# A fused Perceiver kernel: another order of TensorE's work where two batches meet, and small products widened to the full array

## The reference, cut to what matters

```
x = layer_norm(image_embeds, ln1_g, ln1_b)      # 16 x 1601 x 128
l = layer_norm(latents, ln2_g, ln2_b)           # 16 x 64 x 128
q = l @ Wq;  kv_in = concat([x, l], axis=1);  k, v = split(kv_in @ Wkv)
w = softmax(q k^T * scale)                      # 16 heads, 64 x 1665 per head
out = (w @ v) @ Wo                              # back to 64 x 128
```

## Time and profile before

| | |
|---|---|
| Median of 3 runs | 1007.68 us (1007.14 to 1007.98) |
| Profiled execution, its own time | 1005.16 us |
| Its span, first to last instruction | 1003.4 us |
| TensorE busy | 936.7 us, 93% |
| VectorE busy | 760.4 us, 76% |
| ScalarE busy | 720.4 us, 72% |
| GpSimd busy | 376.7 us, 38% |
| Mean granted TensorE clock | 0.976 |

### The profile page before, as it was taken

One profiled execution on the slowest core, in us unless ns is written; L12 is line 12 of the kernel. 1 busy time (PEld: TensorE's weight loads), 2 busy tenths in 40 slices (PEclk: granted clock), 3 DMA queues, 4 the chain that ended last, 5 costly groups with the idle time before them and its releaser, 6 DMA issues.

```text
span 1003.4 us, 20455 instructions
## 1 busy us (share of the span) xinstructions
PE 936.7 (93%) x8246; PEld 488.8 (49%) x8246; DVE 760.4 (76%) x1556; ACT 720.4 (72%) x1033; POOL 376.7 (38%) x376
## 2 busy tenths in 40 slices
PE   8679999999999999999999999999999999979975
PEld 5434444444444444545454545454545444457752
DVE  5968796969696969696969696969695856568965
ACT  4577778787878787878787878787878676645631
POOL 6471133333433333333333334333333222244343
PEclk9799999999999999999999999999999999989987
DMA  6211030203120203020312031202120100000000
GB/s 203 68 27 52 12 79 13 78 13 78 14 76 15 77 15 75 16 75 17 74 18 72 19 73 17 74 18 73 18 61 18 39 2 22 1 23 23 2 6 16
DMA packets 74566, 41.95 MB, mean 42 GB/s; under 512 B 62277, under 2 KB 69865, under 8 KB 74473
## 3 DMA queue, kind: packets, MB, share of 16 engines
q1 hardware_dynamic: 74184, 39.60, 16.3%
q10 hardware_dynamic: 288, 1.05, 0.3%
HBM read 25.98 MB, written 0.59 MB: 26 GB/s over the span
## 4 chain that ended last, share of the span: by engine, by line
PE 56%; DVE 29%; ACT 8%; issue 5%; POOL 1%; DMA 1%; POOLq 0%; ACTq 0%; DVEq 0%
DVE mx L1457 8%; DVE region L1469 7%; PE S L2066 6%; PE WW L2012 6%; PE OA L2099 6%; PE S L2075 6%; PE S L2069 6%; PE OA L2102 6%; PE OA L2105 6%; DVE region L1448 4%; ACT S L1781 2%; ACT region L1777 2%; ACT region L1801 2%; PE WW L2039 1%; PE WW L2041 1%
## 5 line engine op out<-in xcount | busy, mean ns | idle before, releaser
L1469 DVE TENSOR_TENSOR region<-S,region 128x1024 f16<-128x1024 f32 x208 | 252.8, 1215 | 139.1 <-ACT S L1781 139.0
L1777 ACT ACTIVATE region<-S,sigma 128x1024 f16<-128x1024 f32 x208 | 232.6, 1118 | 131.6 <-PE S L2075 130.4
L1457 DVE TENSOR_REDUCE mx<-WW 128x1 f32<-128x512 f32 (+1 forms) x480 | 259.7, 584 | 42.0 <-PE WW L2012 37.6
L1781 ACT ACTIVATE S<-S,sigma 128x1024 f32<-128x1024 f32 x208 | 226.2, 1088 | 0.0
L2066 PE MATMUL S<-region,xT 128*128 128x512 f16 (+1 forms) x416 | 124.5, 381 | 6.0 <-DVE region L1469 4.7
L2012 PE MATMUL WW<-xT,region 128*128 128x512 f16 x360 | 121.3, 382 | 6.2 <-DVE region L1448 3.7
L2075 PE MATMUL S<-region,xT 128*128 128x512 f16 (+1 forms) x416 | 125.0, 382 | 0.0
L2099 PE MATMUL OA<-region,xk 128*128 128x512 f16 (+1 forms) x416 | 124.9, 382 | 0.0
L2102 PE MATMUL OA<-region,xk 128*128 128x512 f16 (+1 forms) x416 | 124.6, 381 | 0.0
L2069 PE MATMUL S<-region,xT 128*128 128x512 f16 (+1 forms) x416 | 124.5, 381 | 0.0
L2105 PE MATMUL OA<-region,xk 128*128 128x512 f16 (+1 forms) x416 | 123.8, 379 | 0.0
(11 more groups left out here) (310 smaller groups left out, 1783.3 us busy)
## 6 DMA issues: line engine op xcount, KB each, us to landing
raw<-ctx SPq DMA_DIRECT2D x16, 768.0 KB
rb<-inv_dram SPq DMA_DIRECT2D x16, 512.0 KB, 3.6
xT<-xk SPq DMA_TRANSPOSE x48, 3.1
left_row<-left_pT SPq DMA_DIRECT2D x48, 2.0 KB
raw<-ctx SPq DMA_DIRECT2D x16, 32.5 KB
WO_lo<-L_xattn_Wq ACTq DMA_DIRECT2D x1, 512.0 KB, 3.6
WO_hi<-L_xattn_Wkv ACTq DMA_DIRECT2D x1, 512.0 KB, 4.6
lx<-x SPq DMA_DIRECT2D x1, 512.0 KB, 6.5
```

The costliest lines, as they stand in the source:

```text
L1457: nc.vector.tensor_reduce(mx[:, r, c:c + 1], W[BANK[("m", n)]][:, 0:width], AX.X, ALU.max)\
L1469: nc.vector.tensor_tensor(p_lo[k], src, p_hi[k], ALU.subtract).then_inc(lo_done.sem, 1)
L1777: nc.scalar.activation(p_hi[k], src, ACT.Exp, scale=sigma[:, 0:1])
L1781: nc.scalar.activation(src, src, ACT.Exp, scale=sigma[:, 0:1]).then_inc(e_done.sem, 1)
```

## The change

TensorE's order where batches meet becomes: scores 12, `mt`, weigh 10, weigh 11 | scores 0 of the next batch, weigh 12 | scores 1, `pj` of the batch before the one just ended | scores 2, `lf`, weigh 0. So `pj` of batch b-2 stands in unit 1 of slot b instead of in unit 12 of slot b-1. `lf` and `lt` become early items (before `weigh`, not after), `lt` ahead of the two last `q`, and the side banks' parity moves with them. The copies of the side banks' outputs go from ScalarE in unit 1 to VectorE in unit 0, ahead of `low_part(b, 0)`. Four kinds of small products get full operands padded with zeros: `ones16` (1 x 64) becomes `first_row` (128 x 64, ones in row 0), `left_p` 128 x 128 instead of 128 x 16, `left_row` and `left_x` 128 rows instead of 3, and the weights of `mt` one column of `m16` repeated 128 times. VectorE clears the padding once, at the start. `queries_low`, the low halves of the queries, stays on VectorE. ScalarE's `outputs` and the latents' copies get an explicit wait for `o_split` of the batch before. The last slot keeps its own order in unit 12.

```diff
--- before.py
+++ after.py
@@ -87,19 +87,19 @@
 
 
 PLAN = [([], []),
-        ([], []),
-        ([], [("lf", 0)]),
+        ([], [("pj", 0)]),
+        ([("lf", 0)], []),
         ([("q", 0), ("q", 1)], some(0, 2)),
         (some(2, 2), some(4, 2)),
-        ([("q", 2), ("q", 3)], some(6, 1) + [("lt", 0)]),
+        ([("lt", 0), ("q", 2), ("q", 3)], some(6, 1)),
         (some(7, 2), some(9, 2)),
         (some(11, 2), some(13, 2)),
         (some(15, 2), some(17, 2)),
         (some(19, 2), some(21, 2)),
         (some(23, 2), some(25, 2)),
         (some(27, 2), some(29, 3)),
-        ([("mt", 0), ("mt", 1)], [("pj", 0)])]
-LATENTS_AT = 1
+        ([("mt", 0), ("mt", 1)], [])]
+LATENTS_AT = 0
 
 
 def bank_of_items():
@@ -140,7 +140,7 @@
         ident = sb("ident", [128, 128])
         ident16 = sb("ident16", [128, 128], F16)
         ones = sb("ones", [128, 128])
-        ones16 = sb("ones16", [1, 64], F16)
+        first_row = sb("first_row", [128, NQ], F16)
         rcol = sb("rcol", [128, 8])
         rinv = sb("rinv", [128, 8])
         rb = sb("rb", [128, COLS])
@@ -203,10 +203,10 @@
 
         left_s = sb("left_s", [128, 8])
         left_e = sb("left_e", [128, 8])
-        left_p = sb("left_p", [128, 16], F16)
+        left_p = sb("left_p", [128, 128], F16)
         left_pT = sb("left_pT", [16, 128], F16)
-        left_row = sb("left_row", [3, COLS], F16)
-        left_x = [sb(f"left_x{p}", [3, D], F16) for p in range(2)]
+        left_row = sb("left_row", [128, COLS], F16)
+        left_x = [sb(f"left_x{p}", [128, D], F16) for p in range(2)]
         srow = sb("srow", [1, COLS])
         attnT = sb("attnT", [128, B * NQ])
 
@@ -489,6 +489,13 @@
             eng.wait_ge(oa_free.sem, oa_free.upto(turn))
             eng.wait_ge(free["ol"].sem, free["ol"].upto(turn, 1))
             vec.tensor_tensor(srow[:], o_sb[0:1, 0, :], o_sb[0:1, 1, :], ALU.add).then_inc(srow_done.sem, 1)
+
+        def latent_outputs(eng, copy, turn):
+            eng.wait_ge(pv_done.sem, pv_done.upto(turn, LAT))
+            if turn.off > 0:
+                eng.wait_ge(o_split.sem, o_split.upto(turn.plus(-1), 1))
+            for k in range(2):
+                copy(o_sb[:, 1, k * HALF:(k + 1) * HALF], W[BANK[("ol", k)]]).then_inc(free["ol"].sem, 1)
 
         def normalise_outputs(eng, vec, turn):
             for k in range(2):
@@ -958,7 +965,7 @@
                 ins = nc.scalar.copy(Vb[t.off % 2][r, :, :, a, 0:2 * SD], v[r])
             ins.then_inc(ta["vb"].sem, 1)
 
-        def tail_scalar(act, outputs, latent_outputs, outputs_high, projected):
+        def tail_scalar(act, outputs, outputs_high, projected):
             def exp(t, k):
                 act.wait_ge(ta["shifted"].sem, ta["shifted"].upto(t, k))
                 e = E[t.off % 2][:, 2 * k:2 * k + 2].rearrange("p g c k n -> p (g c k n)")
@@ -1007,7 +1014,7 @@
 
             exp(Turn(0), 0)
             outputs(LAST)
-            latent_outputs(LAST)
+            latent_outputs(act, nc.scalar.copy, LAST)
             exp(Turn(0), 1)
             for m in range(TB):
                 t = Turn(m)
@@ -1346,7 +1353,12 @@
             nc.vector.memset(stc[:], 0.0)
             nc.vector.memset(mx[:].rearrange("p r c -> p (r c)"), -3e38)
             dve.wait_ge(warm.sem, 1)
-            link(nc.vector.memset(ones16[:], 1.0))
+            nc.vector.memset(left_row[:], 0.0)
+            nc.vector.memset(left_p[:], 0.0)
+            for p in range(2):
+                nc.vector.memset(left_x[p][:], 0.0)
+            link(nc.vector.memset(first_row[:], 0.0))
+            link(nc.vector.memset(first_row[0:1, :], 1.0))
 
             dve.wait_ge(gains_t.sem, 1)
             link(nc.vector.tensor_copy(gb[:], OA[:, 0, 0:4]))
@@ -1490,6 +1502,8 @@
                             maxima(nxt, k)
                         if kind == "lf":
                             left_scores(b)
+                    if u == LATENTS_AT and post:
+                        latent_outputs(dve, nc.vector.tensor_copy, b.plus(-1))
                     if u == LEFT_LOW_AT:
                         left_low_part(b)
                     if u == RECIPROCALS_AT and post:
@@ -1793,13 +1807,9 @@
 
             def outputs(turn):
                 act.wait_ge(pv_done.sem, pv_done.upto(turn, LAT))
+                if turn.off > 0:
+                    act.wait_ge(o_split.sem, o_split.upto(turn.plus(-1), 1))
                 nc.scalar.copy(o_sb[:, 0, :], OA[:].rearrange("p a n -> p (a n)")).then_inc(oa_free.sem, 1)
-
-            def latent_outputs(turn):
-                act.wait_ge(pv_done.sem, pv_done.upto(turn, LAT))
-                for k in range(2):
-                    nc.scalar.copy(o_sb[:, 1, k * HALF:(k + 1) * HALF], W[BANK[("ol", k)]])\
-                      .then_inc(free["ol"].sem, 1)
 
             def projected(turn):
                 act.wait_ge(pe_item["pj"].sem, pe_item["pj"].upto(turn))
@@ -1807,14 +1817,14 @@
                 nc.scalar.activation(dst, side_out(("pj", 0), turn)[:, 0:NQ], ACT.Copy, scale=wscale[:, 1:2])\
                   .then_inc(free["pj"].sem, 1)
 
-            def side_item(item, nxt, old, prep, post):
+            def side_item(item, nxt, old, prep):
                 kind, k = item
                 if kind == "q" and prep:
                     queries_high(nxt, k)
                 if kind == "mt" and prep:
                     shift_row(nxt, k)
-                if kind == "pj" and post:
-                    projected(old)
+                if kind == "pj" and old.off > 0:
+                    projected(old.plus(-1))
 
             def slot(b, prep=True, post=True, stats=True):
                 nxt, old = b.plus(1), b.plus(-1)
@@ -1826,20 +1836,21 @@
                         lambdas_scalar(act)
                     exponentials_high(b, u)
                     for item in early:
-                        side_item(item, nxt, old, prep, post)
+                        if item[0] == "lt":
+                            left_turned(b)
+                        else:
+                            side_item(item, nxt, old, prep)
                     if u == LEFT_EXP_AT:
                         left_exponentials(b)
                     exponentials_full(b, u)
                     if u == 0 and post:
                         outputs(old)
-                    if u == LATENTS_AT and post:
-                        latent_outputs(old)
                     if u in OUTPUTS_HIGH_AT and post:
                         outputs_high(old, OUTPUTS_HIGH_AT[u])
                     for item in late:
-                        side_item(item, nxt, old, prep, post)
-                        if item[0] == "lt":
-                            left_turned(b)
+                        side_item(item, nxt, old, prep)
+                    if b is LAST and u == LAT:
+                        projected(old)
                     if b is LAST and u == H_AT:
                         early_columns_out(act)
                     if b is LAST and u == TILE0_AT:
@@ -1886,7 +1897,7 @@
             slot(Turn(B - 2), stats=False)
             slot(LAST, prep=False, stats=False)
 
-            tail_scalar(act, outputs, latent_outputs, outputs_high, projected)
+            tail_scalar(act, outputs, outputs_high, projected)
 
 
         @block.tensor
@@ -2024,12 +2035,12 @@
                     pe.wait_ge(left_low.sem, left_low.upto(turn))
                     if turn is LAST:
                         pe.wait_ge(x1_read.sem, 1)
-                    ins = mm(w[0:16, 0:128], left_p[:], ident16[:], start=True, stop=True)
+                    ins = mm(w[:, 0:128], left_p[:], ident16[:], start=True, stop=True)
                 if kind == "mt":
                     pe.wait_ge(m16_done.sem, m16_done.upto(turn))
                     for j in range(4):
-                        ins = mm(w[0:1, 128 * j:128 * j + 128], m16[:, 4 * k + j:4 * k + j + 1], ident16[:],
-                                 start=True, stop=True)
+                        ins = mm(w[:, 128 * j:128 * j + 128], m16[:, 4 * k + j:4 * k + j + 1].to_broadcast([128, 128]),
+                                 ident16[:], start=True, stop=True)
                 if kind == "pj":
                     pe.wait_ge(o_split.sem, o_split.upto(turn, 1))
                     for n in range(2 * H):
@@ -2069,7 +2080,7 @@
                         mm(banks[r, k, :], hi, q_lo[p][:, cols(qc, k)], start=False, stop=False)
                 if u == LAT:
                     for k in range(2):
-                        mm(banks[KEPT:128, k, :], ones16[:], q_hi[p][0:1, cols(0, k)], start=False, stop=False)
+                        mm(banks[KEPT:128, k, :], first_row[:], q_hi[p][:, cols(0, k)], start=False, stop=False)
                 for k in range(2):
                     for r, hi, lo, qc in keys_of:
                         ins = mm(banks[r, k, :], lo, q_hi[p][:, cols(qc, k)], start=False, stop=True)
@@ -2122,25 +2133,24 @@
                         elif item[0] in PREP:
                             if prep:
```

(17 more changed lines are left out.)

## The result

| | before | after |
|---|---|---|
| median of 4 runs | 1007.41 us (1006.53 to 1007.98) | 989.34 us (988.93 to 989.81) |
| ratio, 95% interval | | 0.9822 [0.9804, 0.9839] |
| span of the profiled execution | 1003.4 us | 988.1 us |
| its own time | 1005.16 us | 989.81 us |
| one slot (from one outputs' copy on ScalarE to the next, mean of the steady ones) | 50.07 us | 49.15 us |

The change gains 18.1 us.

A forecast was written before the change was run, and what follows sets the result against it. TensorE's instruction stream bounds the kernel, so holes in it count. Terms 3.0 + 3.3 + 1.5 + 8.3 - 3.6 - 0.75 - 1.3 = 10.45 us, from 1007.68 to 997.2 us; range 991 to 1004.

The forecast's parts named there:

- left-over token, two changes of shape: Weighing of the left-over token on TensorE: 128 rows remove two shape changes, 0.19 us a slot, 3.0 us over 16 slots.
- `first_row`: TensorE's `first_row` product, made 128 x 64 like its neighbours: 0.22 us of holes go, 3.3 us over 15 slots.
- `mt`: TensorE's eight `mt` products: the shape change behind them goes, 0.10 us in 15 slots, 1.5 us.
- `lf`'s two holes: TensorE's holes before and after `lf`, 0.27 + 0.28 = 0.55 us, both go in slots 1 to 15: 8.3 us.
- `lt`: old holes less new: `lt` ahead of the last `q`: old holes 0.47 us, new waits 0.71, a cost of 3.6 us over 15 slots.
- weigh 12's wait: Weigh 12 on TensorE waits for `low_part` 12: about even, taken as 0.05 us, 15 times, a cost of 0.75 us.
- period near 49.4: Sign that the forecast is right: about 49.4 us between outputs' copies on ScalarE, against 50.07 before.
- the copies on VectorE: Copies moved to VectorE ahead of `low_part(b, 0)`: taken as 1.28 us, leaving 1.5 us of slack before scores 2.
- Slot 1's hole: Before scores 2 in slot 1, with no batch to project: a TensorE hole of 1.3 us, once.
- The rival of slow loads: Repeated columns load slowly in `mt`: 0.34 us, 15 times, 5.2 us lost, so 1002.4 us; chance 0.15.
- The slower rival: Weigh 12 as new wait: chain from scores 12 to `low_part` 12 over 5.6 us; at 5.75, 1011.7 us; chance 0.06.
- More gain: `q` 3 hides half its wait, 5 us less, 992.2 us, or all of it, 987.3; chance 0.07.

The follow-up runs named there:

- h_before: The kernel before with all seven of VectorE's tile passes of the last slot in unit 6, ahead of GpSimd's products; median 1001.99 us, ratio 0.9967.
- after_again: The kernel after, unchanged, timed again in five more runs; median 989.59 us, ratio 0.9831 to the kernel before.
- lt_later: The kernel after with `lt` moved behind `q` 2 and 3 in unit 5, ScalarE's copy of it too; median 988.09 us, ratio 0.9823 to the kernel before.
- shapes_only: The kernel before with the padded operands alone, its order kept; median 996.36 us, ratio 0.9909.

## Where the prediction was right, and where it failed

Terms of one slot (us), by the starts on TensorE. Each is measured up to the next start at full pace, so the 0.01 us by which the pair behind a change of shape is late counts too:

| term | forecast | measured |
|---|---|---|
| left-over token, two changes of shape | 0.19 | 0.21 |
| `first_row` | 0.22 | 0.23 |
| `mt` | 0.10 | 0.09 |
| `lf`'s two holes | 0.55 | 0.62 |
| `lt`: old holes less new | 0.47 - 0.71 | 0.49 - 0.76 |
| weigh 12's wait | -0.05 | 0 |
| hole between weigh 3 and the maxima, not forecast | | 0.04 |
| sum | 0.77 | 0.92 |
| slot by the period | "near 49.4", 0.67 less | 0.91 |

The recorded "period near 49.4" doesn't follow from the terms, which give 50.07 - 0.77 = 49.30.

- **Right:** each mechanism that was forecast. Changes of shape at 0.1 us; `lf`'s bank wait gone; ScalarE's exponential ahead of `lt`'s copy as the next wait; the copies on VectorE at 1.29 us (I took 1.28) with 1.58 us to spare (1.5); weigh 12 even with `low_part` 12, whose chain stayed 4.70 us (459.72 less 455.02, the last start of scores 12). Slot 1's hole is 1.28 us (1.3).
- **The rival of slow loads** is out: the loads of `mt` take 98 ns each as `pj`'s do, and eight of them fit into 0.46 us with their matmuls. The Trainium skill (TensorE: Matmul & The Clock Gate, section "What overlaps and what doesn't") lets a load overlap only with matmuls in other row groups; the trace disagrees, since the eight loads and matmuls of `mt` all use all 128 rows, and eight times 98 ns would be 0.78 us. **The slower rival** needed a chain of over 5.6 us and found 4.70. **More gain** by `q` 3 hiding its wait did not come: it waits 0.71 in full. That 989.34 lies between the two times given for that rival (992.2 and 987.3) is chance.

In the median, the forecast was 997.2 - 989.34 = 7.9 us too high. The miss has these parts, by the profiled executions, with the start of weigh 12 on TensorE as the marker:

1. *The steady slots*: the stretch of slots 1 to 14 shrank by 14.3 us; the terms gave 12.3 (14 x 0.77, plus 2.8 for the `pj` that left slot 1, less 1.3). That is 2.0 us, some 0.15 a slot: 0.07 at `lf`, whose 16 matmuls take 0.41 us and not the 0.46 that I took, 0.05 at weigh 12, 0.04 ahead of the maxima.
2. *The last slot*: 4.04 us instead of 0.74, so 3.3. The step that failed is the count "slots 1 to 15" itself: I priced the last slot as if it were one of the others and never read its own waits. Its wait of 2.41 us for `h` was a row of the trace of before, and it was not looked at because the change doesn't touch it. The change moved its phase. 1.04 us came from a tile pass that no longer met a product, 1.69 from the clock, 0.24 because the holes around `lf` are 0.79 us in this slot and not 0.55 (the one behind it is a wait for VectorE's `left_s`), 0.19 from `lt`, whose two changes of shape go without a new wait here, 0.10 behind the left-over token, where the change of shape had held up the second of eight small products, and 0.04 from smaller differences. `h_before` shows the first two without any other change.
3. *Start and end*: 0.4 us the other way. The first weigh 12 comes 0.27 us earlier (117.20 against 117.47), near the 0.22 that the terms give slot 0, and the stretch to the end is 0.5 us longer, where I had nothing.
4. *The distance to the median*: I kept 2.5 us between the profiled execution and the median. The profiled execution before was one of the quicker ones; that of after lies 0.5 us above its median. That is 3.0 us, the second largest part, and it comes from the spread of the executions: against the later medians of the same two kernels (1006.13 and 989.59) the distances are 1.0 and -0.2 us. The runs of `h_before` show the size of the spread: those with a mean granted clock of 0.974 to 0.977 took 1000.75 to 1002.66 us, the three with 0.972 took 1005.59 to 1006.78. One of these three was profiled, and its slots are those of the kernel before at a clock of 1.00, so its time was lost outside them. The mean clock is not all of it: three runs of `after_again` with 0.977 took 986.20, 986.68 and 989.59 us.

2.0 + 3.3 - 0.4 + 3.0 is 7.9.

Open: why the wait of 2.57 us before the transposes was followed by a stretch at half clock in the kernel before and that of 2.56 us in `lt_later` was not. One execution of each was profiled, so it may be the phase or the execution, and that the wait made the clock fall is not shown. The stretch to the end varies from 130.9 to 135.3 us between kernels whose code there is the same, and its length follows its granted clock: 0.89 in the profile of before and in both of after (130.9 to 131.4 us), 0.88 and 0.87 where it takes 132.4 to 133.2, and 0.86 in that of `h_before`, 135.3 us. By these figures TensorE stood at half clock for some 9 us more in `h_before` than in before, an estimate that gives the 4.4 us between them. What sets the clock there is open; it took back part of the gain of `lt_later`, `shapes_only` and `h_before` in their profiles.

## What to carry to other kernels

Count holes from starts, at every change of operand shape and every bank handed over, then price the first, second and last stages from their own rows: a shift of 0.2 us can decide there whether two passes collide. When a copy stands between two users of a bank, put it on the engine whose queue has nothing long ahead of it at that moment; here, ScalarE or VectorE in unit 0, that alone was worth 1 us a slot. A period is best read on the engine that is the bound: a marker on another engine can move against it, here by 0.60 us. Forecast from profile to profile, and allow for the spread of the executions instead of carrying over the distance of one of them.

## What was unexpected of the hardware

- A VectorE pass of 128 x 128 that takes 0.34 us alone took 1.29 to 1.37 us when it met a GpSimd product of 1.26 us on other data, in steps of one whole product: waits for `h` of 2.57, 1.53 and 0 us for two, one and no pass met.
- A load of one column repeated 128 times costs what a load of 128 columns does, 98 ns, and its matmuls stream at full pace (eight in 0.46 us).
- A load of weights starts a whole place (0.21 us) ahead of its matmul where the shape stays, and only with it where the shape changes; the hole there is 0.1 us.
- A wait of TensorE can be followed by a second loss: behind 2.57 us of idle time in the kernel before, 1.69 us went at the lower clock. In `lt_later` a wait of 2.56 us at the same place had nothing behind it.
